# A two-layer graph attention kernel: the same steps of every engine in another order, and PSUM banks by another list

## The reference

```python
def _L0_gnn_ref(seq_inputs, Wq, bq, Wk, bk, Wv, bv, Wf, bf, graph_mask):   # 6 heads of 64
    q, k, v = _heads(seq_inputs @ Wq + bq), _heads(seq_inputs @ Wk + bk), _heads(seq_inputs @ Wv + bv)
    scores = jnp.einsum('bhqd,bhkd->bhqk', q, k) / np.sqrt(HEAD_SIZE)
    probs = jax.nn.softmax(scores + jnp.where(graph_mask, 0.0, NEG)[:, None], axis=-1)
    ctx = jnp.einsum('bhqk,bhkd->bhqd', probs, v)
    return ctx.transpose(0, 2, 1, 3).reshape(...) @ Wf + bf
def _L1_gnn_ref(feat_in, adj, W, b, w_src, w_dst, H_w, H_b):               # 12 heads of 32
    h = jnp.einsum('bnd,ade->bane', feat_in, W)
    th = jnp.tanh(h)
    attn = jnp.einsum('bane,aeo->bano', th, w_src) + jnp.swapaxes(jnp.einsum('bane,aeo->bano', th, w_dst), 2, 3)
    attn = jnp.where(attn >= 0, attn, LEAKY_ALPHA * attn)
    attn = jax.nn.softmax(jnp.where(mask, jnp.float32(-999.0), attn), axis=-1)
    feat_out = jax.nn.elu(jnp.einsum('banm,bame->bane', attn, h) + b)      # heads side by side
    gate = jax.nn.sigmoid(feat_in @ H_w.T + H_b)
    return gate * feat_out + (1.0 - gate) * feat_in
x = _layernorm(x + _L0_gnn_ref(x, ..., adj), axis=-1)
x = _layernorm(x + _L1_gnn_ref(x, adj, ...), axis=-1)
```

## Time and profile before

| | before |
|---|---|
| time of the runs, us: median (lowest to highest) | 1122.04 (1121.91 to 1124.87), 3 runs |
| span of the profiled execution, us | 1121.2 |
| PE busy, us (share of the span) | 1047.1 (93%) |
| DVE | 1025.2 (91%) |
| POOL | 947.2 (84%) |
| ACT | 893.5 (80%) |

### The profile page before, as it was taken

One profiled execution on the slowest core, in us unless ns is written; L12 is line 12 of the kernel. 1 busy time (PEld: TensorE's weight loads), 2 busy tenths in 40 slices (PEclk: granted clock), 3 DMA queues, 4 the chain that ended last, 5 costly groups with the idle time before them and its releaser, 6 DMA issues.

```text
span 1121.2 us, 32794 instructions
## 1 busy us (share of the span) xinstructions
PE 1047.1 (93%) x10890; PEld 950.8 (85%) x10890; DVE 1025.2 (91%) x2138; ACT 893.5 (80%) x1739; POOL 947.2 (84%) x781
## 2 busy tenths in 40 slices
PE   4899999999999999999999999999999999999761
PEld 4888889889898988889898888889888888988641
DVE  5589999999999999999999999999999999999854
ACT  4568888888888888888888888888888888888753
POOL 2158889988888998888899888889988888998775
PEclk9899999999999999999999999999999999999975
DMA  6103333232333333234333323433332243332232
GB/s 200 32 21 73 98 84 89 76 86 66 82 97 83 89 79 84 70 79 97 83 89 81 82 74 74 97 83 89 83 82 77 69 97 83 93 81 72 47 67 73
DMA packets 188717, 91.33 MB, mean 81 GB/s; under 512 B 158864, under 2 KB 183696, under 8 KB 188688
## 3 DMA queue, kind: packets, MB, share of 16 engines
q1 hardware_dynamic: 188688, 90.95, 32.7%
HBM read 31.61 MB, written 12.58 MB: 39 GB/s over the span
## 4 chain that ended last, share of the span: by engine, by line
PE 73%; issue 9%; DVE 8%; POOL 4%; ACT 3%; DMA 1%; DVEq 0%; SPq 0%; POOLq 0%; ACTq 0%
PE lin L459 42%; PE zp L554 6%; PE zp L613 3%; PE zp L617 3%; PE fp L583 3%; PE tp L498 3%; PE tp L567 3%; PE tp L626 2%; DVE sd L1008 2%; PE tp L595 2%; PE fp L586 2%; PE fp L640 2%; ACT th L736 1%; ACT sd_t L765 1%; POOL z L1353 1%
## 5 line engine op out<-in xcount | busy, mean ns | idle before, releaser
L1353 POOL TENSOR_TENSOR z<-z,z_max 128x1536 f32<-128x1536 f32 x64 | 176.4, 2757 | 21.3 <-DVE z_max L1136 18.9
L818 ACT ACTIVATE z<-z,log_scale 128x1536 f32<-128x1536 f32 x64 | 101.3, 1583 | 53.7 <-POOL z L1353 53.6
L1360 POOL TENSOR_TENSOR p_lo<-z,p_hi 128x1024 f16<-128x1024 f32 x64 | 137.3, 2145 | 2.3 <-ACT p_hi L824 2.3
L1365 POOL TENSOR_TENSOR f<-f,x_kept 128x384 f32<-128x384 f32 x64 | 65.0, 1016 | 72.0 <-DVE f L1168 72.0
L1318 POOL TENSOR_TENSOR prod<-th,w_sd_rows 128x768 f32<-128x768 f32 x64 | 117.9, 1842 | 6.6 <-ACT th L736 6.4
L784 ACT ACTIVATE p<-p,p_min 128x128 f32<-128x128 f32 x384 | 118.9, 399 | 4.7 <-DVE p_min L1068 4.7
L1129 DVE SCALAR_TENSOR_TENSOR z<-zp,z 128x1536 f32<-128x1536 f32 x64 | 111.9, 1748 | 2.3 <-ACT z L793 2.3
L1136 DVE TENSOR_REDUCE z_max<-z 128x12 f32<-128x1536 f32 x64 | 111.6, 1744 | 0.1
L793 ACT ACTIVATE z<-zp 128x1536 f32<-128x1536 f32 x64 | 93.2, 1457 | 17.8 <-PE zp L617 17.8
L1331 POOL TENSOR_TENSOR v_part<-v_res,v_part 128x384 bf16<-128x384 f32 x64 | 63.0, 984 | 35.8 <-ACT v_part L755 33.8
L459 PE MATMUL lin<-xt_hi,Wq_hi 128*128 128x256 f32 x288 | 81.0, 281 | 12.7 <-DVE Wk_lo L926 12.4
(11 more groups left out here) (162 smaller groups left out, 4394.2 us busy)
## 6 DMA issues: line engine op xcount, KB each, us to landing
xt_raw<-x_t SPq DMA_DIRECT2D x32, 384.0 KB, 4.0
x_raw<-x SPq DMA_DIRECT2D x32, 384.0 KB, 3.2
x_kept<-x SPq DMA_DIRECT2D x64, 192.0 KB, 2.3
out<-out_tile SPq DMA_DIRECT2D x64, 192.0 KB, 1.9
adj<-adj SPq DMA_DIRECT2D x64, 32.0 KB, 1.9
dst_row<-sd_t SPq DMA_DIRECT2D x64, 9.0 KB
p1t_hi<-p_hi SPq DMA_TRANSPOSE x64, 3.2
p1t_lo<-p_lo SPq DMA_TRANSPOSE x64, 3.1
```

What stands on the lines that cost most here:

```text
L818: act.activation(z[:, g, :], z[:, g, :], ACT.Exp, bias=log_scale[:, :]).then_inc(z_exp[g].sem, 1)
L1353: pool.tensor_tensor(zs, zs, z_max[:, g, :].unsqueeze(2).to_broadcast([128, H1, N]), ALU.subtract)\
L1360: pool.tensor_tensor(p1_lo[:, g, :], z[:, g, PE_HEADS * N:], p1_hi[:, g, :], ALU.subtract).then_inc(w1_lo[g].sem, 1)
```

## The change

Each engine makes the same instructions, in another order, and the lists of PSUM users and banks follow. A step may now also be written two turns late (`later`) or one turn early (`early`), and one more turn is written out ahead of the loop. In the diff, many lines move from the end of a body to its start with `step` turned into `late`, or the other way: such a step keeps its place on the circle, and only the point at which the loop begins is another.

```diff
+    def shifted(self, turns, stage, function, *which):
+
+        if self.runs(stage, turns):
+            self.behind = turns
             function(*which)
             self.behind = 0
 
+    def late(self, stage, function, *which):
+        self.shifted(1, stage, function, *which)
+
+    def later(self, stage, function, *which):
+        self.shifted(2, stage, function, *which)
...
-TP_USERS = ("x1t1", "pt00", "pt01", "sdt", "pt10", "pt11", "ct0", "ct1", "wt0", "x1t0", "wt1")
-FP_USERS = ("f0", "f1", "ctx0", "ctx1")
...
+TP_USERS = ("pt10", "sdt", "pt11", "ct0", "ct1", "wt0", "x1t0", "x1t1", "wt1", "pt00", "pt01")
+FP_USERS = ("f1", "ctx0", "ctx1", "f0")
...
@@ TensorE
-                turn.late(1, x1_transposes, 1)
-                turn.late(0, scores, 1)
-                turn.late(2, attend1, 0, 0)
-                turn.late(2, attend1, 0, 1)
-                turn.late(2, attend1, 0, 2)
-                turn.late(1, hidden, 1)
-                turn.late(0, weights0_transposes, 0, 0)
-                turn.late(0, weights0_transposes, 0, 1)
-                turn.late(1, gate_rows, 0)
                 turn.step(0, queries_keys, 0)
                 turn.late(2, attend1, 1, 0)
                 turn.late(2, attend1, 1, 1)
-                turn.late(1, source_target_transposes)
                 turn.late(2, attend1, 1, 2)
                 turn.late(0, weights0_transposes, 1, 0)
+                turn.late(1, source_target_transposes)
+                turn.late(0, attend0, 0)
                 turn.late(0, weights0_transposes, 1, 1)
-                turn.late(0, attend0, 0)
+                turn.late(0, context_transposes, 0)
                 turn.late(1, attention1, 0)
-                turn.late(0, context_transposes, 0)
                 turn.late(0, attend0, 1)
-                turn.step(0, values, 0)
                 turn.late(0, project, 0)
                 turn.late(0, context_transposes, 1)
+                turn.step(0, values, 0)
                 turn.late(1, attention1, 1)
...
                 turn.step(1, hidden, 0)
+                turn.step(1, x1_transposes, 1)
                 turn.step(2, weights1_transposes, 1)
+                turn.step(0, scores, 1)
+                turn.step(2, attend1, 0, 0)
+                turn.step(1, hidden, 1)
+                turn.step(2, attend1, 0, 1)
+                turn.step(2, attend1, 0, 2)
+                turn.step(0, weights0_transposes, 0, 0)
...
@@ ScalarE
+                turn.late(1, source_target_copy)
+                turn.late(0, weights0_high, 1, 0)
...
+                turn.later(1, gate_tanh, 1)
...
@@ VectorE
                 turn.late(1, z_maxima, 1)
-                turn.late(2, stats1, 0)
                 turn.late(0, shift_norm0, 0)
...
@@ GpSimd
+                turn.late(2, features_difference, 0)
+                turn.late(2, gated_features, 0)
+                turn.late(1, mask1_bias)
+                turn.late(1, hidden_low, 0)
+                turn.late(0, value_part3, 1)
...
@@ SyncE
+                turn.late(1, turn_weights1_low, 0)
+                turn.late(0, load_adj1)
+                turn.late(1, turn_weights1_high, 1)
                 turn.late(-1, load_x)
```

More of the change, by code:

```diff
@@ L84, in step, with early @@
             function(*which)
-    def late(self, stage, function, *which):
-        if self.runs(stage, 1):
-            self.behind = 1
+    def shifted(self, turns, stage, function, *which):
+        if self.runs(stage, turns):
+            self.behind = turns
             function(*which)
             self.behind = 0
+    def early(self, stage, function, *which):
+        self.shifted(-1, stage, function, *which)
+    def late(self, stage, function, *which):
+        self.shifted(1, stage, function, *which)
+    def later(self, stage, function, *which):
+        self.shifted(2, stage, function, *which)
     def starts(self, stage):
@@ L112, in turns @@
     counts = set()
-    for t in range(-1, 4):
+    for t in range(-1, 5):
         body(Turn(eng, t, passed, counts))
@@ L873, in body @@
                 turn.step(-1, next_x_high)
+                turn.late(0, norm0, 1)
                 turn.step(0, value_part1, 1)
-                turn.late(0, norm0, 1)
                 turn.step(1, hidden_tanh, 0)
-                turn.step(2, turned1_high, 1)
                 turn.step(1, x1_high, 1)
                 turn.late(1, weights1_high, 1)
+                turn.step(2, turned1_high, 1)
                 turn.step(0, scores_exp, 0)
@@ L1209, in body @@
                 turn.late(0, context_low, 1)
+                turn.step(0, value_residue, 0)
                 turn.late(0, stats0, 0)
@@ L1252, in body @@
                 turn.step(1, source_target_part1)
+                turn.late(2, shift_norm1, 0)
                 turn.step(1, source_target_residue)
-                turn.step(1, source_target_part2)
-                turn.step(1, source_target_part3)
-                turn.step(2, elu, 0)
                 turn.late(2, shift_norm1, 1)
-                turn.step(2, features_inverse, 1)
-                turn.step(2, features_norm, 1)
             turns(dve, passed, body, first_biases)
@@ L1386, in body @@
                 turn.late(1, z_subtract, 0)
+                turn.late(0, deviation0, 0)
                 turn.step(0, value_part3, 0)
+                turn.step(0, mask0_bias)
                 turn.late(2, mix, 1)
-                turn.late(0, deviation0, 0)
-                turn.step(0, mask0_bias)
                 turn.late(1, z_subtract, 1)
+                turn.late(0, deviation0, 1)
                 turn.late(1, weights1_low, 0)
-                turn.late(0, deviation0, 1)
-                turn.late(2, deviation1, 0)
                 turn.step(-1, next_x_low)
@@ L1398, in body @@
                 turn.step(1, source_target_products, 1)
+                turn.late(2, deviation1, 0)
                 turn.late(2, deviation1, 1)
-                turn.step(1, mask1_bias)
-                turn.step(2, features_difference, 0)
-                turn.step(0, value_part3, 1)
-                turn.step(2, gated_features, 0)
             turns(pool, passed, body, biases_loaded)
```

103 lines of the change are left out of this document (52 added, 51 removed).

## The result

| | before | changed |
|---|---|---|
| time of the runs, us: median (lowest to highest) | 1122.81 (1121.91 to 1124.87), 4 runs | 1145.20 (1142.81 to 1147.11), 4 runs |
| ratio, 95% interval | | 1.0201 (1.0183 to 1.0220) |
| span of the profiled execution, us | 1121.2 | 1143.0 |
| turn in the loop, us | 32.65 | 33.51 |

The account below looks back on a forecast made before the run. TensorE was taken to bound the turn: 0.67 + 0.70 - 0.99 = +0.38 us, 11.4 over 30 turns, plus 1.2 for the last turns and 0.8 around the span, gave 1134.6 us. Range 1118 to 1146, its own 1128 to 1144.

Parts of the forecast that it names:

- The wait of attend0 for f_norm, +0.67: TensorE between attend1 of graph 1 and attend0 of graph 0: 1.17 us chain, less covered work, leaves 0.67 per turn.
- the last part comes a few tenths of a microsecond later: VectorE's last sd part: slightly later, but TensorE asks for it 0.64 us later, so nothing booked.
- The wait for the context, +0.70: Graph 0's context transposes on TensorE: 1.04 us chain covered by only 0.34 of p transposes; 0.70 instead of 0.08.
- The old waits, -0.99: TensorE's four present waits per turn (sd, sd_t, context and x1 transposes: 0.29 + 0.47 + 0.08 + 0.15) all go.
- The one at the x1 transposes: TensorE's 0.15 us wait goes because VectorE's shift_norm0 of graph 0 no longer follows a 0.55 us statistics step.
- The projection's cover: TensorE's projection loses values as cover for context_high and context_low; attention1 (1.30) and attend0 (0.91) remain; nothing booked.
- The last turn, +1.2: GpSimd's mask1 behind features_difference and gated_features ends the last turn's mask and row copy 1.2 us later, once.
- The time around the span, +0.8: Median of the runs lies 0.8 us above the profiled span; added at the end to 1133.8 us.
- the slowest rival: VectorE's features_negative of graph 1 is held by a GpSimd step: 0.43 per turn, 13 us more, 1147.5; chance 0.10.
- Faster: Rival: p transposes' wait belongs to sd_t, f_norm is ready for attend0; -0.29 per turn, 1114.5 us; chance 0.14.
- No change, since VectorE sets the turn: Rival: VectorE's work and gaps already fill 32.66 us, absorbing TensorE's new waits; 1122 to 1125 us; chance 0.13.

Follow-up runs that it names:

- z0_first: Changed kernel with attention1 of graph 0 put back ahead of the context transposes of graph 0 on TensorE: 1156.85 us, ratio 1.0299.
- before_stats_moved: Kernel before with only VectorE's statistics step of graph 0 (second norm) moved behind shift_norm0 of graph 0: 1123.46 us, ratio 1.0010.
- context_behind_mask: Kernel of cut_moved_mask_between with, on TensorE for graph 0, attention1 ahead of the context transposes and values ahead of the projection, readers following: 1152.38 us.
- dve_cut_moved: Changed kernel with VectorE's loop cut where it was before, behind features_norm of graph 1, order on the circle unchanged: 1152.20 us, ratio 1.0269.
- cut_moved_mask_between: Changed kernel with VectorE's loop cut where it was before and GpSimd's mask1 between features_difference and gated_features of graph 0: 1140.05 us, ratio 1.0152.
- only_tensor_order: Kernel before with TensorE's new order and the new lists of banks and users alone: 1393.00 us, ratio 1.2413.

## Why the forecast was right in direction and short in size

- **The wait of attend0 for f_norm, +0.67.** The wait is there, but is 1.00: 1.50 between attend1 and attend0, less 0.03 + 0.34 + 0.13. This is the mis-sized term. The step that failed is "the last part comes a few tenths of a microsecond later, while TensorE asks for it 0.64 later ...: nothing booked". Even sdt waits a little, 0.23 us (0.57 behind the first half of p, 468.31 to 468.88, of which 0.34 is work), which lies inside attend0's wait. What counts is that the reciprocal and f_norm stand behind that part in VectorE's list, and attend0 waits for them. The text also took the cut of the loop for a matter of writing ("only the point at which the loop begins is another", of the part on the change), where it costs 0.36 us of idle time in the middle of the chain. Before, the jump lay behind f_norm, whose 0.62 us cover it: f_neg starts 0.13 us behind f_norm's end, 0.03 now, but it does so in the loop's first turn too, ahead of any jump (133.85). So 0.25 of the 0.33 are the jump, which makes the reciprocal late, and 0.10 are the step to f_norm, which is longer inside this kernel's loop for a reason that stays open. With the cut back there and the GpSimd collision out of the way both go, and 1.16 was measured.
- **The wait for the context, +0.70.** Measured 0.71. What the forecast did not see is that it can't be had back by the swap alone: the flat rows are as late, for sdt had gone behind attend1, and attention1's mask stands behind gated_features. Put ahead with the mask in time, attention1 waits 0.65 itself.
- **The old waits, -0.99.** sdt's, the p transposes' and the context's (0.84) went. The one at the x1 transposes went too: from the first weight transpose to the values it is 0.22 less (0.90 to 0.68). But its reason was wrong. The statistics step moved alone brings nothing, because ScalarE's p_hi holds x. In the changed kernel p_hi ends 1.1 us ahead of x (450.15 plus 1.06, x at 452.32); that ScalarE's new list is what freed the transposes is likely, but was not tested by itself.
- **The projection's cover.** Nothing was booked and nothing was lost in the changed kernel; the run z0_first showed how thin it is, 0.34 us at once.
- **Not in the forecast:** the second and third queries-keys block, 0.15 us longer (below). The sum is then 1.00 + 0.71 - 0.84 - 0.22 + 0.15 = 0.80 per turn, where 0.86 was measured.
- **The last turn, +1.2.** It is there: the last row products start 10.30 us behind the last sdt (1102.20 to 1112.50), 8.99 before (1080.06 to 1089.05), 1.3 us more. But the time from the last first part of sd to the end of the span is the same, 42.3 us, and the turn ahead of it is 2.9 us shorter (31.06 against 33.96). Where that comes from was not looked into. Besides, the first queries-keys block started 1.2 us earlier in this execution (11.14 us against 12.38; in the other runs 11.1 to 12.5). These two are why the span grew by no more than 21.8 us.
- **The time around the span, +0.8.** It set the median of several runs against the span of one of them. Where a run's time and span are both on record, 1.7 to 3.3 us lie between them, mostly 2.0; this makes 1.4 us of the miss.
- **The range.** The measured 1145.2 lies inside 1118 to 1146 partly by luck. The forecast's own range ended at 1144 (0.7 per turn, where 0.86 was measured), and what lies above was added for the slowest rival, which did not happen. Its lower end adds up to 1129, not 1128.
- **The rivals.** Faster: no, f_norm ends 1.45 us behind attend1. No change, since VectorE sets the turn: half of it is true. VectorE's chain from sd to the context is now on the chain of work that ended last (VectorE has 17% of it, 8% before), but it lengthens the turn instead of hiding the waits. Slowest, f_neg held by GpSimd: not in the changed kernel, where it takes 0.36 us in every full turn. It holds in the closest neighbours: moving the changed kernel's cut by five steps, or in the kernel before attend0 by one, makes a VectorE step (f_neg there, elu here) 0.8 us longer or more in the turns where GpSimd starts first. The chance of 0.10 was low for a mechanism that decides by hundredths of a microsecond; what kept it away here is the order, as far as these runs tell.

No version beat the kernel before. The closest, before_stats_moved, is the same within what can be told.

## What to carry to other kernels

When a step moves in a list, price what stands behind it on its own engine and is waited for elsewhere, not only the step itself; and look at where the loop is cut, because here a jump in the middle of a chain of short dependent steps showed in full (0.36 us idle), while an instruction of 0.62 us ahead of it hid it. A wait that is removed tells only which of several late chains was last: here the mask (z0_first), the context (the changed kernel) and the flat rows (context_behind_mask) let TensorE go on 1.8, 2.0 and 2.6 us behind the start of attend0, so undoing one swap moved the wait and did not remove it. Orders that several engines share can't be tested one engine at a time.

## What the runs showed of the hardware that was not expected

- VectorE's jump back costs 0.36 us of idle time behind a step of 0.21 us. Behind one of 0.62 us nothing of it shows: the 0.13 us there is the same in the loop's first turn, ahead of any jump.
- VectorE and GpSimd steps that read SBUF and start within some nanoseconds of each other have two outcomes, with 1.5 us between two turns of the same loop: VectorE's f_neg waited where GpSimd's step started 7 to 12 ns ahead, and GpSimd's step was stretched where it started from 5 ns ahead to 14 behind (dve_cut_moved and cut_moved_mask_between).
- The 36 matmuls of the second and third queries-keys blocks start 0.1133 us apart before (439.21 to 443.18 for 35 steps) and 0.1178 now (448.86 to 452.98), evenly from the first to the last and at a granted clock of 1.00 (2.4 GHz); the first block has 0.118 in both. In only_tensor_order both spacings occur in different turns. Moving TensorE's cut changed nothing. In context_behind_mask, which has TensorE's swaps at the context and the values undone, it is 0.1133 to 0.1138 again in all its steady turns; z0_first, with the first of the two swaps undone, has 0.1178. It costs 0.15 us a turn, and its cause stays open.
